# Loads on one ring, stores on another, and the variance moved ahead, in a wavelet pyramid on a group-normalised image

## The chip, the cores and the metric

The kernel runs on one core of a Trainium2 chip. The metric is device time in microseconds, lower is better: the median of three runs of the kernel before is 1376.59 us (1376.27 to 1378.16). The changed kernel is timed on the same chip beside it.

## The reference

The input `x` is float32 of shape 8 x 32 x 512 x 512. Each image is group-normalised with 16 groups, so that a group is two neighbouring channels: mean and variance over 2 x 512 x 512 elements, epsilon 1e-5. A three-level low-pass pyramid of the normalised image is added to `x`:

```python
def _wavelet_pyramid(x, levels=3):
    k1 = jnp.array([0.25, 0.5, 0.25])
    K = jnp.outer(k1, k1)[None, None]
    result = x
    for level in range(levels):
        sh, sw = (H // 2 ** level, W // 2 ** level)
        temp = result[:, :, :sh, :sw].reshape(B * C, 1, sh, sw)
        approx = conv(temp, K, stride 1, padding SAME)
        down = approx[:, :, ::2, ::2]
        result = result.at[:, :, :sh // 2, :sw // 2].set(down)
    return result

x = x + _wavelet_pyramid(_gn(x))
```

Each level smooths the top-left corner left by the level before with a 3 x 3 kernel, takes every second row and column, and writes that into the corner's own top-left quarter. Outside the 256 x 256 corner the output is therefore `x` plus its normalised self, a scaling by (1 + r) with a bias, where r is the reciprocal standard deviation; inside, `x` plus a level of the pyramid.

## The kernel before, in words

There are 128 groups of two channels (2.097 MB each). All of a group lies in one of eight slots of `xs` in SBUF: 128 partitions, each with eight rows of 512 elements (2 channels, 2 halves of the image called top and bottom, 2 rows per partition), ordered half first, then channel, then row. The groups run in laps of eight, one group a step. In step u an engine's program holds work of three groups: u itself, u - 1 (`LAG`) and u - 2 (`LAG_L3`). Each engine has its order written out by hand in its `step`, and semaphores tie the engines together.

SyncE (lines 131 to 159) carries all transfers on one ring, as DMAs of 1 MB, half a group each. At the start it issues the loads of all eight slots. Then for each group k: it waits until ScalarE has scaled the bottom half (`scaled`), stores it (L136), waits for the two VectorE additions (`l1_added`, `l2_added`), stores the top half (L139), and issues the two loads (L145) of the group six further on, once the slot's former group is stored.

VectorE, in its step: L309 forms 2 x even + odd columns of the new group into `h1` (semaphore `h1_part`); `rstd` (L273, L274) takes the reciprocal of the standard deviation of the group before and frees its variance bank; L315 adds the left neighbours into `h1` and accumulates the row sums (`h1_ready`); L321 adds row pairs into `a1`; `add_corner` (L296, twice) adds the pyramid's corner of group u - 2 out of PSUM; `add_level1` (L284 and L285) adds level 1 of group u - 1 at the right and below.

TensorE, in its step: `mean` (L346 to L348, which wait for `h1_ready`); `level3` of group u - 2 (L397 to L400); `level1` of group u, eight matmuls (L361 to L369); `variance` (L376), which needs ScalarE's sum of squares; `level2` of group u - 1 (L387 to L389). Matmuls are float32, and each of them shows as two records in the trace.

ScalarE, in its step: `moments` (L433 turns the mean in PSUM into the negative mean, L438 squares the whole group and accumulates), `evacuate1` (L449 and L450, level 1 from PSUM to `l1`), `root` (L458, standard deviation), `scale_beside` (L472) and `scale_bottom` (L477) of group u - 1, `evacuate2` (L465).

GpSimd refines r by one Newton step (`coefs`, L223 to L234), which gives the scaling's coefficients, and corrects the first column of `l1` after its evacuation (L256).

Of the kernel before, what the change touches and what calls it, by code (L numbers as in the profile page):

```python
# [16 lines left out]
SLOTS = 8  # L17
LAG = 1
LAG_L3 = 2
AHEAD = 6  # L20


def pyramid_kernel(nc: bass.Bass, x: bass.AP, out: bass.AP):
# [7 lines left out]


    def groups(a):
        return a.rearrange("b (g c) (f p s) w -> (b g) p c f (s w)", c=CG, f=HALVES, s=RPP)

    x_dram = groups(x).rearrange("(l k) p c f n -> l k f p c n", k=SLOTS)
    out_dram = groups(out).rearrange("(l k) p c f n -> l k f p c n", k=SLOTS)

    with ExitStack() as ctx:
        def sb(name, shape, dt=F32):  # L40
# [8 lines left out]

        xs = sb("xs", [P, SLOTS, ROWS * W])  # L50
        h1 = sb("h1", [P, 2, ROWS, W1])
        a1 = sb("a1", [P, 2, HALVES, CG, W1])
        l1 = sb("l1", [P, 2, CG, RPP, W1])
        l2 = sb("l2", [P, 2, CG, W2])
        squares = sb("squares", [P, ROWS * W], BF16)
# [69 lines left out]
        def rows(slot):  # L125
            return xs[:, slot, :].rearrange("p (r w) -> p r w", w=W)

        def half_of(slot, f):
            return xs[:, slot, :].rearrange("p (f c n) -> p f c n", c=CG, f=HALVES)[:, f]

        @block.sync
        def _(sp):
            def store(lap, k):
                n = lap * SLOTS + k
                sp.wait_ge(scaled, n + 1)
                sp.dma_start(out_dram[lap, k, 1], half_of(k, 1)).then_inc(x_stored[k], 16)  # L136
                sp.wait_ge(l1_added, n + 1)
                sp.wait_ge(l2_added, n + 1)
                sp.dma_start(out_dram[lap, k, 0], half_of(k, 0)).then_inc(x_stored[k], 16)  # L139

            def load(lap, slot):
                if later(lap, 0, 1):
                    sp.wait_ge(x_stored[slot], 16 * HALVES * lap)
                for f in range(HALVES):
                    sp.dma_start(half_of(slot, f), x_dram[lap, slot, f]).then_inc(x_loaded[slot], 16)  # L145

            def step(lap, k, last=False):
                store(lap, k)
                if later(lap * SLOTS, k, SLOTS - AHEAD) and not (last and k + AHEAD >= SLOTS):
                    load(lap + (k + AHEAD) // SLOTS, (k + AHEAD) % SLOTS)  # L150

            for k in range(SLOTS):
                load(0, k)
            for lap in range(LAPS):
                for k in range(SLOTS):
                    step(lap, k, last=lap == LAPS - 1)

            for slot in range(SLOTS):
                sp.wait_ge(x_stored[slot], 16 * HALVES * LAPS)

        @block.gpsimd
        def _(pool):
# [104 lines left out]
        def _(dve):  # L267
# [8 lines left out]
            def add_level1(base, k):  # L276
                b = k % 2
                d = slice(b, b + 1)
                top = rows(k % SLOTS)[:, 0:TOP]
                l1v = l1[:, b].rearrange("p c s w -> p (c s) w")  # L280
                dve.wait_ge(r_ready, base + k + 1)
                dve.wait_ge(l1_fixed, base + k + 1)
                right, below = top[:, :, W2:W1], top[HP:P, :, 0:W2]
                nc.vector.scalar_tensor_tensor(right, l1v[:, :, W2:W1], r[:, d], right, ALU.mult, ALU.add)  # L284
                nc.vector.scalar_tensor_tensor(below, l1v[HP:P, :, 0:W2], r[HP:P, d], below, ALU.mult,  # L285
                                               ALU.add).then_inc(l1_added, 1)

            def add_corner(base, k):
                b = k % 2
                d = slice(b, b + 1)  # L290
                img = rows(k % SLOTS)[:, 0:TOP].rearrange("p (c s) w -> p c s w", s=RPP)
                dve.wait_ge(l3_ps_ready, base + k + 1)
                for s in range(RPP):
                    level = l2_ps[b][HP * s:HP * (s + 1), 0:CG * W2].rearrange("p (c w) -> p c w", c=CG)
                    corner = img[0:HP, :, s, 0:W2]
                    last = nc.vector.scalar_tensor_tensor(corner, level, r[0:HP, d], corner, ALU.mult, ALU.add)  # L296
                last.then_inc(l2_added, 1)

            def step(lap, u):
                base = lap * SLOTS  # L300
                b = u % 2
                k = u - LAG
                make = exists(base, u)
                if make:
                    dve.wait_ge(x_loaded[u], 16 * HALVES * (lap + 1))
                    if later(base, u, 2):
                        dve.wait_ge(l1_ps_ready, base + u - 1)
                    v = rows(u)
                    nc.vector.scalar_tensor_tensor(h1[:, b], v[:, :, 0:W:2], 2.0, v[:, :, 1:W:2], ALU.mult,  # L309
                                                   ALU.add).then_inc(h1_part, 1)  # L310
                if exists(base, k):
                    rstd(base, k)
                if make:
                    dve.wait_ge(h1_part, base + u + 1)
                    nc.vector.scalar_tensor_tensor(h1[:, b, :, 1:W1], v[:, :, 1:W - 2:2], 1.0, h1[:, b, :, 1:W1],  # L315
                                                   ALU.mult, ALU.add,
                                                   accum_out=hsum[:, b:b + 1]).then_inc(h1_ready, 1)
                    dve.wait_ge(h1_ready, base + u + 1)
                    hp = h1[:, b].rearrange("p (i s) w -> p i s w", s=RPP)
                    av = a1[:, b].rearrange("p f c w -> p (f c) w")  # L320
                    nc.vector.scalar_tensor_tensor(av, hp[:, :, 0], 2.0, hp[:, :, 1], ALU.mult,  # L321
                                                   ALU.add).then_inc(a1_ready, 1)
                if exists(base, u - LAG_L3):
                    add_corner(base, u - LAG_L3)
                if exists(base, k):
                    add_level1(base, k)
# [10 lines left out]
        def _(pe):  # L337
            pe.wait_ge(consts_ready, 1)

            def mean(base, u):  # L340
                b = u % 2
                pe.wait_ge(h1_ready, base + u + 1)
                if later(base, u, 1):
                    pe.wait_ge(negm_ready, base + u)
                dst = mean_ps[:, 0:ROWS]
                nc.tensor.matmul(dst, mean_w[:], h1[:, b, :, 0], start=True, stop=False)  # L346
                nc.tensor.matmul(dst, mean_w[:], rows(u)[:, :, W - 1], start=False, stop=False)  # L347
                nc.tensor.matmul(mean_ps[:, 0:1], mean_w[:], hsum[:, b:b + 1], start=False,  # L348
                                 stop=True).then_inc(mean_ready, 1)

            def level1(base, u):
                b = u % 2
                hv = h1[:, b].rearrange("p (f c s) w -> p f c s w", f=HALVES, s=RPP)
                av = a1[:, b]
                even, odd = l1_ps[b][:, 0], l1_ps[b][:, 1]
                even_t, even_b, odd_t, odd_b = even[0:HP], even[HP:P], odd[0:HP], odd[HP:P]
                prev, mid, nxt = w1_prev[:, 0:HP], w1_even[:, 0:HP], w1_odd[:, 0:HP]
# [8 lines left out]
                nc.tensor.matmul(odd_b, mid, hv[:, 1, :, 1], start=True, stop=False)  # L366
                nc.tensor.matmul(odd_t, nxt, av[:, 0], start=False, stop=True)  # L367
                nc.tensor.matmul(even_b, mid, av[:, 1], start=False, stop=True)  # L368
                nc.tensor.matmul(odd_b, nxt, av[:, 1], start=False, stop=True).then_inc(l1_ps_ready, 1)  # L369

            def variance(base, u):
# [31 lines left out]
            def step(lap, u):  # L403
                base = lap * SLOTS
                if exists(base, u):
                    mean(base, u)
                if exists(base, u - LAG_L3):
                    level3(base, u - LAG_L3)
                if exists(base, u):
                    level1(base, u)  # L410
                    variance(base, u)
                if exists(base, u - LAG):
                    level2(base, u - LAG)

# [9 lines left out]
        def _(act):  # L424
# [43 lines left out]
            def scale_beside(base, k):  # L468
                c = slice(k % 2, k % 2 + 1)
                act.wait_ge(coef_ready, base + k + 1)  # L470
                beside = rows(k % SLOTS)[:, 0:TOP, W1:W]
                nc.scalar.activation(beside, beside, ACT.Identity, bias=negmr[:, c], scale=r_plus1[:, c])  # L472

            def scale_bottom(base, k):
                c = slice(k % 2, k % 2 + 1)
                bottom = xs[:, k % SLOTS, TOP * W:ROWS * W]
                nc.scalar.activation(bottom, bottom, ACT.Identity, bias=negmr[:, c],  # L477
                                     scale=r_plus1[:, c]).then_inc(scaled, 1)

            def step(lap, u):  # L480
                base = lap * SLOTS
                make, done = exists(base, u), exists(base, u - LAG)
                if make:
                    moments(base, u)
                    evacuate1(base, u)
                    root(base, u)
                if done:
                    scale_beside(base, u - LAG)
                    scale_bottom(base, u - LAG)
                    evacuate2(base, u - LAG)  # L490

            for lap, u in HEAD:
                step(lap, u)
# [19 lines left out]
```

## Time and profile before

| | |
|---|---|
| median of three runs | 1376.59 us |
| the profiled execution, its own time | 1377.61 us |
| its span (first to last instruction) | 1375.9 us |
| moved by DMA | 537.08 MB, 390 GB/s over the span |
| packets | 139280; 131072 of 4 KB carry the data |
| granted TensorE clock, mean | 0.996 |

The busy time of an engine as a share of the span says how full it is, not whether it is the limit. A wait names the engine that waited, the line it was about to run, and the instruction that ended the wait. The chain of waits is followed back from the last instruction, so an engine that shows on it in a stretch set the pace there. The windows give for a stretch each engine's busy time with its number of instructions, the granted clock, the mean busy share of the 16 DMA engines (it can be a little over 1, because packets of an engine overlap slightly) and the GB/s they moved.

### The profile page before, as it was taken

How to read it: one execution, taken by the hardware profiler on the slowest of the kernel's cores; microseconds unless marked ns; L12 is line 12 of the kernel's file. 1: busy time of each engine (PE TensorE's matmuls, PEld its weight loads, DVE VectorE, ACT ScalarE, POOL GpSimd, SP SyncE). 2: the span in 40 equal slices, each digit the busy share in tenths (PEclk: the TensorE clock that was granted, in tenths of full speed). 3: DMA queues.
4: the chain of work that ended last, by engine and by line, in shares of the span. 5: the costliest groups of instructions: out<-in, count | busy, mean ns of one | idle time of the engine just before them, and what ended most of it. 6: DMA issues, size and time to landing. Idle time of an engine off the chain costs nothing.

```text
span 1375.9 us, 18859 instructions
## 1 busy us (share of the span) xinstructions
PE 1229.0 (89%) x5632; PEld 692.5 (50%) x5632; DVE 1077.1 (78%) x1280; ACT 1138.6 (83%) x1282; POOL 598.7 (44%) x1316
## 2 busy tenths in 40 slices
PE   4989998998999899989989998999899899989997
PEld 1555455455545554554555455555545554555554
DVE  4787877878787878778787878787787878787874
ACT  3888888888888888888888888888888888888886
POOL 4444444444444444444444444444444444444442
PEclk9999999999999999999999999999999999999999
DMA  9799999999999999999999999999999999999976
GB/s 382 300 401 398 401 395 401 399 398 401 398 403 394 403 398 399 397 401 398 397 401 400 402 394 402 400 399 398 401 400 397 401 399 400 397 400 398 400 316 244
DMA packets 139280, 537.08 MB, mean 390 GB/s; under 512 B 8192, under 2 KB 8192, under 8 KB 139264
## 3 DMA queue, kind: packets, MB, share of 16 engines
q1 hardware_dynamic: 139264, 536.90, 99.6%
q8 instruction: 5, 0.08, 0.0%
q14 instruction: 11, 0.09, 0.0%
HBM read 268.44 MB, written 268.44 MB: 390 GB/s over the span
## 4 chain that ended last, share of the span: by engine, by line
PE 60%; DVE 23%; ACT 9%; issue 7%; DMA 1%; ACTq 0%; DVEq 0%; SPq 0%
DVE h L315 20%; PE l_ps L362 9%; PE l_ps L361 8%; PE l_ps L369 8%; PE l_ps L365 8%; PE l_ps L367 8%; ACT l L450 6%; PE l_ps L397 4%; PE mean_ps L346 4%; PE l_ps L398 2%; PE mean_ps L347 2%; PE l_ps L399 2%; PE l_ps L400 2%; PE mean_ps L348 2%; ACT std L458 2%
## 5 line engine op out<-in xcount | busy, mean ns | idle before, releaser
L438 ACT ACTIVATE squares<-xs,negm 128x4096 bf16<-128x4096 f32 x128 | 475.0, 3711 | 4.2
L256 POOL TENSOR_TENSOR l<-l,col_fix 128x4 f32<-128x4 f32 x128 | 28.3, 221 | 688.4 <-ACT l L450 688.4
L309 DVE SCALAR_TENSOR_TENSOR h<-xs 128x2048 f32<-128x2048 f32 x128 | 293.7, 2295 | 12.2 <-DMA xs<-x_dram 8.3
L315 DVE SCALAR_TENSOR_TENSOR h<-xs,h 128x2040 f32<-128x2040 f32 x128 | 291.0, 2274 | 0.0
L223 POOL TENSOR_TENSOR newt<-r 128x1 f32<-128x1 f32 x128 | 270.5, 2113 | 37.1 <-DVE ve L274 37.1
L477 ACT ACTIVATE xs<-xs,negmr,r_plus 128x2048 f32<-128x2048 f32 x128 | 268.0, 2094 | 0.0
L449 ACT ACTIVATE l<-l_ps,negm_e 128x512 f32<-128x512 f32 x128 | 87.9, 687 | 190.3 <-PE l_ps L369 190.3
L296 DVE SCALAR_TENSOR_TENSOR xs<-l_ps,r,xs 64x256 f32<-64x256 f32 x256 | 123.0, 480 | 109.6 <-PE l_ps L400 107.8
L346 PE MATMUL mean_ps<-h,mean_w 128*128 128x8 f32 x256 | 50.1, 268 | 138.1 <-DVE h L315 138.1
L321 DVE SCALAR_TENSOR_TENSOR a<-h 128x1024 f32<-128x1024 f32 x128 | 157.0, 1227 | 4.4
L472 ACT ACTIVATE xs<-xs,negmr,r_plus 128x1024 f32<-128x1024 f32 x128 | 159.7, 1247 | 0.0
L273 DVE RECIPROCAL r<-std 128x1 f32<-128x1 f32 x128 | 21.0, 164 | 162.8 <-ACT std L458 162.8
L226 POOL TENSOR_TENSOR newt<-newt,ve 128x1 f32<-128x1 f32 x128 | 147.8, 1154 | 0.0
L362 PE MATMUL l_ps<-h,w_even 128*64 128x512 f32 x256 | 139.0, 625 | 0.0
L363 PE MATMUL l_ps<-h,w_prev 128*64 128x512 f32 x256 | 139.0, 625 | 0.0
L346 PEld LDWEIGHTS mean_ps<-h,mean_w 128*128 128x128 f32 x256 | 38.5, 189 | 191.1 <-DVE h L315 178.1
L361 PE MATMUL l_ps<-h,w_prev 128*128 128x512 f32 x256 | 133.1, 602 | 0.0
L365 PE MATMUL l_ps<-a,w_even 128*64 128x512 f32 x256 | 131.9, 597 | 0.0
L366 PE MATMUL l_ps<-h,w_even 128*64 128x512 f32 x256 | 131.8, 597 | 0.0
L367 PE MATMUL l_ps<-a,w_odd 128*64 128x512 f32 x256 | 130.7, 592 | 0.0
L368 PE MATMUL l_ps<-a,w_even 128*64 128x512 f32 x256 | 130.7, 592 | 0.0
L369 PE MATMUL l_ps<-a,w_odd 128*64 128x512 f32 x256 | 130.7, 592 | 0.0
(83 smaller groups left out, 2300.6 us busy)
## 6 DMA issues: line engine op xcount, KB each, us to landing
xs<-x_dram SPq DMA_DIRECT2D x256, 1024.0 KB, 10.4
y_dram<-xs SPq DMA_DIRECT2D x256, 1024.0 KB, 7.3
```

Of the source, the lines that this page charges most:

```text
L223: nc.gpsimd.tensor_tensor(newt[:, b, 0:1], r0[:, c], r0[:, c], ALU.mult).then_inc(newt_step, 1)
L309: nc.vector.scalar_tensor_tensor(h1[:, b], v[:, :, 0:W:2], 2.0, v[:, :, 1:W:2], ALU.mult, ALU.add).then_inc(h1_part, 1)
L315: nc.vector.scalar_tensor_tensor(h1[:, b, :, 1:W1], v[:, :, 1:W - 2:2], 1.0, h1[:, b, :, 1:W1], ALU.mult, ALU.add, accum_out=hsum[:, b:b + ...
L321: nc.vector.scalar_tensor_tensor(av, hp[:, :, 0], 2.0, hp[:, :, 1], ALU.mult, ALU.add).then_inc(a1_ready, 1)
L361: nc.tensor.matmul(even, w1_prev[:], hv[:, 0, :, 1], start=True, stop=False)
L362: nc.tensor.matmul(odd_t, mid, hv[:, 0, :, 1], start=True, stop=False)
L365: nc.tensor.matmul(even_t, mid, av[:, 0], start=False, stop=True)
L367: nc.tensor.matmul(odd_t, nxt, av[:, 0], start=False, stop=True)
L369: nc.tensor.matmul(odd_b, nxt, av[:, 1], start=False, stop=True).then_inc(l1_ps_ready, 1)
L438: nc.scalar.activation(squares[:], xs[:, u % SLOTS, :], ACT.Square, bias=negm[:, b:b + 1], accum_out=sumsq[:, b:b + 1]).then_inc(sumsq_rea ...
L472: nc.scalar.activation(beside, beside, ACT.Identity, bias=negmr[:, c], scale=r_plus1[:, c])
L477: nc.scalar.activation(bottom, bottom, ACT.Identity, bias=negmr[:, c], scale=r_plus1[:, c]).then_inc(scaled, 1)
```

## The change

All loads stay on SyncE's ring, and a group is loaded by one DMA of 2 MB; SyncE does nothing else. A group is stored by one DMA of 2 MB, which ScalarE issues on its own ring at the end of its step, two steps after the group's load was used; it waits for the scaling and both VectorE additions. The rows in a slot are ordered channel first, then half, then row, as in DRAM, so views of a half are now strided and `add_level1` needs two instructions where it had one. On TensorE the variance matmul goes ahead of the last level 1 matmul, and two of the three mean lines wait for `h1_part` in place of `h1_ready`. On ScalarE the scaling beside and the root go ahead of `evacuate1`.

```diff
-        return a.rearrange("b (g c) (f p s) w -> (b g) p c f (s w)", c=CG, f=HALVES, s=RPP)
+        return a.rearrange("b (g c) (f p s) w -> (b g) p (c f) (s w)", c=CG, f=HALVES, s=RPP)
...
-        a1 = sb("a1", [P, 2, HALVES, CG, W1])
+        a1 = sb("a1", [P, 2, CG, HALVES, W1])
...
+        def top_of(slot):
+            return xs[:, slot, :].rearrange("p (c f s w) -> p f c s w", c=CG, f=HALVES, s=RPP)[:, 0]
+        def whole(slot):
+            return xs[:, slot, :].rearrange("p (h n) -> p h n", n=RPP * W)
...
         def _(sp):
...
             def load(lap, slot):
                 if later(lap, 0, 1):
-                    sp.wait_ge(x_stored[slot], 16 * HALVES * lap)
-                for f in range(HALVES):
-                    sp.dma_start(half_of(slot, f), x_dram[lap, slot, f]).then_inc(x_loaded[slot], 16)
+                    sp.wait_ge(x_stored[slot], 16 * lap)
+                sp.dma_start(whole(slot), x_dram[lap, slot]).then_inc(x_loaded[slot], 16)
             for lap in range(LAPS):
-                for k in range(SLOTS):
-                    step(lap, k, last=lap == LAPS - 1)
+                for slot in range(SLOTS):
+                    load(lap, slot)
...
             def add_level1(base, k):
...
-                nc.vector.scalar_tensor_tensor(right, l1v[:, :, W2:W1], r[:, d], right, ALU.mult, ALU.add)
-                nc.vector.scalar_tensor_tensor(below, l1v[HP:P, :, 0:W2], r[HP:P, d], below, ALU.mult,
-                                               ALU.add).then_inc(l1_added, 1)
+                for s in range(RPP):
+                    right = top[:, :, s, W2:W1]
+                    nc.vector.scalar_tensor_tensor(right, l1v[:, :, s, W2:W1], r[:, d], right, ALU.mult, ALU.add)
+                for s in range(RPP):
+                    below = top[HP:P, :, s, 0:W2]
+                    last = nc.vector.scalar_tensor_tensor(below, l1v[HP:P, :, s, 0:W2], r[HP:P, d], below, ALU.mult,
+                                                          ALU.add)
+                last.then_inc(l1_added, 1)
...
             def mean(base, u):
                 b = u % 2
-                pe.wait_ge(h1_ready, base + u + 1)
+                pe.wait_ge(h1_part, base + u + 1)
...
                 nc.tensor.matmul(dst, mean_w[:], rows(u)[:, :, W - 1], start=False, stop=False)
+                pe.wait_ge(h1_ready, base + u + 1)
                 nc.tensor.matmul(mean_ps[:, 0:1], mean_w[:], hsum[:, b:b + 1], start=False,
...
                 nc.tensor.matmul(even_b, mid, av[:, 1], start=False, stop=True)
+                variance(base, u)
                 nc.tensor.matmul(odd_b, nxt, av[:, 1], start=False, stop=True).then_inc(l1_ps_ready, 1)
...
                     level1(base, u)
-                    variance(base, u)
...
+            def store(lap, k):
+                n = lap * SLOTS + k
+                slot, back = k % SLOTS, k // SLOTS
+                act.wait_ge(scaled, n + 1)
+                act.wait_ge(l1_added, n + 1)
+                act.wait_ge(l2_added, n + 1)
+                nc.scalar.dma_start(out_dram[lap + back, slot], whole(slot)).then_inc(x_stored[slot], 16)
...
                 if make:
                     moments(base, u)
-                    evacuate1(base, u)
-                    root(base, u)
                 if done:
                     scale_beside(base, u - LAG)
+                if make:
+                    root(base, u)
+                    evacuate1(base, u)
+                if done:
                     scale_bottom(base, u - LAG)
                     evacuate2(base, u - LAG)
+                if exists(base, u - LAG_L3):
+                    store(lap, u - LAG_L3)
```

## Rows read from the trace of the kernel before

**Rows 1.** The page: busy time of the engines, and the DMA queue.
```profile
PE 1229.0 (89%) x5632; PEld 692.5 (50%) x5632; DVE 1077.1 (78%) x1280; ACT 1138.6 (83%) x1282; POOL 598.7 (44%) x1316
...
q1 hardware_dynamic: 139264, 536.90, 99.6%
```

**Rows 2.** The waits: who waited for whom, us in total, times, longest.
```profile
ACT l L449 <- PE l_ps L369: 190.3, 128, 2.8
DVE r L273 <- ACT std L458: 162.8, 128, 8.0
PE mean_ps L346 <- DVE h L315: 138.1, 128, 13.1
DVE h L309 <- DMA xs<-x_dram: 8.3, 1, 8.3
```

**Rows 3.** The chain of waits over one period: start us, us, what.
```profile
698.97 2.21 DVE h L315 x2
...
701.22 0.39 PE mean_ps L346 x2
701.61 0.22 PE mean_ps L347 x2
701.83 0.22 PE mean_ps L348 x2
702.05 0.48 PE l_ps L397 x2
...
706.79 0.87 PE l_ps L369 x2
...
708.27 0.68 ACT l L450
708.96 0.16 ACT std L458
...
709.48 2.21 DVE h L315 x2
```

**Rows 4.** The timeline of the same period: start us, us, engine, line.
```profile
702.39 3.71 ACT L438 ACTIVATE squares<-xs,negm 128x4096 bf16<-128x4096 f32 x1
...
708.84 0.26 ACT L458 ACTIVATE std<-var_ps,eps_t 128x1 f32<-128x1 f32 x1
708.99 1.25 ACT L472 ACTIVATE xs<-xs,negmr,r_plus 128x1024 f32<-128x1024 f32 x1
...
710.18 0.61 PE L389 MATMUL l_ps<-l,w_second 128*128 128x254 f32 x2
```

**Rows 5.** Groups of instructions: two VectorE additions, busy us and mean ns.
```profile
L296 DVE SCALAR_TENSOR_TENSOR xs<-l_ps,r,xs 64x256 f32<-64x256 f32 x256 | 123.0, 480 | 109.6 <-PE l_ps L400 107.8
...
L284 DVE SCALAR_TENSOR_TENSOR xs<-l,r,xs 128x512 f32<-128x512 f32 x128 | 94.4, 737 | 0.6 <-POOL r L231 0.6
```

**Rows 6.** Windows; the last three numbers are PEclk, DMA share and GB/s.
```profile
0.00:5.00 5.00, 0.00 (x0) 0.00 (x0) 0.00 (x0) 0.00 (x0) 3.44 (x25) 1.00 0.62 209
...
20.00:25.00 5.00, 1.77 (x8) 0.57 (x4) 0.61 (x3) 2.81 (x4) 0.42 (x2) 1.00 1.03 410
...
55.00:60.00 5.00, 4.40 (x18) 2.54 (x15) 3.82 (x4) 3.70 (x5) 2.04 (x2) 1.00 0.29 112
...
100.00:400.00 300.00, 272.32 (x1259) 154.08 (x1259) 240.65 (x288) 254.15 (x286) 133.95 (x289) 1.00 1.02 399
...
600.00:602.00 2.00, 2.00 (x12) 0.56 (x6) 1.97 (x2) 1.13 (x2) 0.00 (x0) 1.00 1.03 422
602.00:604.00 2.00, 2.00 (x10) 1.29 (x9) 0.92 (x1) 1.37 (x4) 0.00 (x0) 1.00 1.00 344
...
1365.00:1370.00 5.00, 3.97 (x21) 2.98 (x20) 2.88 (x6) 2.37 (x3) 0.00 (x0) 1.00 1.02 403
```

**Rows 7.** Instructions by line: duration ns min/median/max, first and last start.
```profile
L315 DVE SCALAR_TENSOR_TENSOR h<-xs,h x128: 2272/2273/2283, 10.6 to 1350.3; 128x2040 f32<-128x2040 f32 x128
...
L136 SPq DMA_DIRECT2D y_dram<-xs x128: 372/383/388, 39.8 to 1367.0; - x128
...
L145 SPq DMA_DIRECT2D xs<-x_dram x256: 435/932/5488, 0.8 to 1314.6; - x128
```

More of the change, by code:

```diff
@@ L19 @@
 LAG_L3 = 2
-AHEAD = 6
 def pyramid_kernel(nc: bass.Bass, x: bass.AP, out: bass.AP):
@@ L33, in groups @@
     def groups(a):
-        return a.rearrange("b (g c) (f p s) w -> (b g) p c f (s w)", c=CG, f=HALVES, s=RPP)
-    x_dram = groups(x).rearrange("(l k) p c f n -> l k f p c n", k=SLOTS)
-    out_dram = groups(out).rearrange("(l k) p c f n -> l k f p c n", k=SLOTS)
+        return a.rearrange("b (g c) (f p s) w -> (b g) p (c f) (s w)", c=CG, f=HALVES, s=RPP)
+    x_dram = groups(x).rearrange("(l k) p h n -> l k p h n", k=SLOTS)
+    out_dram = groups(out).rearrange("(l k) p h n -> l k p h n", k=SLOTS)
     with ExitStack() as ctx:
@@ L128, in half_of @@
         def half_of(slot, f):
-            return xs[:, slot, :].rearrange("p (f c n) -> p f c n", c=CG, f=HALVES)[:, f]
+            return xs[:, slot, :].rearrange("p (c f n) -> p f c n", c=CG, f=HALVES)[:, f]
+        def top_of(slot):
+            return xs[:, slot, :].rearrange("p (c f s w) -> p f c s w", c=CG, f=HALVES, s=RPP)[:, 0]
+        def whole(slot):
+            return xs[:, slot, :].rearrange("p (h n) -> p h n", n=RPP * W)
         @block.sync
         def _(sp):
[L133 to L139, printed above, removed]
             def load(lap, slot):
                 if later(lap, 0, 1):
-                    sp.wait_ge(x_stored[slot], 16 * HALVES * lap)
-                for f in range(HALVES):
-                    sp.dma_start(half_of(slot, f), x_dram[lap, slot, f]).then_inc(x_loaded[slot], 16)
[L147 to L150, printed above, removed]
-            for k in range(SLOTS):
-                load(0, k)
+                    sp.wait_ge(x_stored[slot], 16 * lap)
+                sp.dma_start(whole(slot), x_dram[lap, slot]).then_inc(x_loaded[slot], 16)
             for lap in range(LAPS):
-                for k in range(SLOTS):
-                    step(lap, k, last=lap == LAPS - 1)
+                for slot in range(SLOTS):
+                    load(lap, slot)
             for slot in range(SLOTS):
-                sp.wait_ge(x_stored[slot], 16 * HALVES * LAPS)
+                sp.wait_ge(x_stored[slot], 16 * LAPS)
         @block.gpsimd
@@ L278, in add_level1 @@
                 d = slice(b, b + 1)
-                top = rows(k % SLOTS)[:, 0:TOP]
-                l1v = l1[:, b].rearrange("p c s w -> p (c s) w")
+                top, l1v = top_of(k % SLOTS), l1[:, b]
                 dve.wait_ge(r_ready, base + k + 1)
                 dve.wait_ge(l1_fixed, base + k + 1)
-                right, below = top[:, :, W2:W1], top[HP:P, :, 0:W2]
-                nc.vector.scalar_tensor_tensor(right, l1v[:, :, W2:W1], r[:, d], right, ALU.mult, ALU.add)
-                nc.vector.scalar_tensor_tensor(below, l1v[HP:P, :, 0:W2], r[HP:P, d], below, ALU.mult,
-                                               ALU.add).then_inc(l1_added, 1)
+                for s in range(RPP):
[6 more added lines that the diff above has]
+                last.then_inc(l1_added, 1)
             def add_corner(base, k):
@@ L290, in add_corner @@
                 d = slice(b, b + 1)
-                img = rows(k % SLOTS)[:, 0:TOP].rearrange("p (c s) w -> p c s w", s=RPP)
+                img = top_of(k % SLOTS)
                 dve.wait_ge(l3_ps_ready, base + k + 1)
@@ L304, in step @@
                 if make:
-                    dve.wait_ge(x_loaded[u], 16 * HALVES * (lap + 1))
+                    dve.wait_ge(x_loaded[u], 16 * (lap + 1))
                     if later(base, u, 2):
@@ L319, in step @@
                     hp = h1[:, b].rearrange("p (i s) w -> p i s w", s=RPP)
-                    av = a1[:, b].rearrange("p f c w -> p (f c) w")
+                    av = a1[:, b].rearrange("p c f w -> p (c f) w")
                     nc.vector.scalar_tensor_tensor(av, hp[:, :, 0], 2.0, hp[:, :, 1], ALU.mult,
@@ L352, in level1 @@
                 b = u % 2
-                hv = h1[:, b].rearrange("p (f c s) w -> p f c s w", f=HALVES, s=RPP)
-                av = a1[:, b]
+                hv = h1[:, b].rearrange("p (c f s) w -> p f c s w", f=HALVES, s=RPP)
+                av = a1[:, b].rearrange("p c f w -> p f c w")
                 even, odd = l1_ps[b][:, 0], l1_ps[b][:, 1]
@@ L470, in scale_beside @@
                 act.wait_ge(coef_ready, base + k + 1)
-                beside = rows(k % SLOTS)[:, 0:TOP, W1:W]
+                beside = top_of(k % SLOTS)[:, :, :, W1:W]
                 nc.scalar.activation(beside, beside, ACT.Identity, bias=negmr[:, c], scale=r_plus1[:, c])
@@ L475, in scale_bottom @@
                 c = slice(k % 2, k % 2 + 1)
-                bottom = xs[:, k % SLOTS, TOP * W:ROWS * W]
+                bottom = half_of(k % SLOTS, 1)
                 nc.scalar.activation(bottom, bottom, ACT.Identity, bias=negmr[:, c],
                                      scale=r_plus1[:, c]).then_inc(scaled, 1)
+            def store(lap, k):
[5 more added lines that the diff above has]
+                nc.scalar.dma_start(out_dram[lap + back, slot], whole(slot)).then_inc(x_stored[slot], 16)
             def step(lap, u):
```

## The prediction

> **What bounds the kernel now.** I read the page first: TensorE is busy 89% of the span, ScalarE 83%, VectorE 78%, and the one DMA queue 99.6% [rows 1]. Two suspects, then: a chain of compute, and the DMA engines. The waits come next, because a bound by loads would show there. VectorE waited for a load once, 8.3 us at the start, and never again; what it, TensorE and ScalarE wait for in every one of the 128 groups is each other [rows 2]. The chain of waits says how: from one L315 to the next it runs through mean, level 3, level 1 on TensorE, then both evacuations (the last is L450) and the root on ScalarE, the reciprocal on VectorE, and back to L315. The two L315 rows stand 10.51 us apart, and no DMA is in between [rows 3]. First and last L315 start at 10.6 and 1350.3 us [rows 7]; 127 periods of 10.51 are 1334.8, so the ramp costs 4.9 more, and 25.6 us follow the last start to the span's 1375.9.
>
> So compute sets the pace. The windows show how little the DMA engines have in reserve, which is the heart of this prediction. A group moves 2.097 MB in and as much out, 4.194 MB. In the steady stretch they move 399 GB/s, that is 10.51 us a group: exactly compute's period. Loads alone ran at 410, stores alone (the end of the run) at 403, the best 2 us windows between at 422, and once a period there is a dip to 344 [rows 6]. Whether 399 is what compute asks for or nearly all that mixed traffic can get, the trace of before cannot tell.
>
> **The change on the compute side.** Two of the three mean matmul lines wait only for L309's half: after L315 there is one line (0.39) where there were 0.39 + 0.22 + 0.22 before level 3 [rows 3], so 0.44 us leaves the chain. The variance matmul goes ahead of L369 and the root ahead of the evacuations. In the times of [rows 3, 4]: squares end at 702.39 + 3.71, plus 0.1 for the accumulator read, 706.2; less 0.44 that is 705.8. TensorE reaches L369's place at 706.79 - 0.44 = 706.35, so the variance waits for nothing and ends near 706.75. ScalarE meanwhile does the scaling beside (1.25 us, to 707.0), then the root (0.26), and the reciprocal pair (0.35) frees L315 at 707.65 in place of 709.48. The chain is 1.83 us shorter: 8.7 us. The scaling needs GpSimd's coefficients of the group before; GpSimd works 598.7/128 = 4.7 us a group [rows 1], and counted from a root one period back it is done some 3 us before ScalarE asks. Its own wait for the evacuation comes behind that and costs nobody.
>
> What is late next is each engine's own work. TensorE: from L346 at 701.22 to the end of L389 at 710.79 without a pause, **9.57 us**; the moved matmuls stay in that sum. ScalarE: a period of 10.51 less its wait of 190.3/128 = 1.49 [rows 2] is 9.02, and now it issues the stores. One issue of 1 MB on SyncE took 0.37 to 0.39 us; the loads' issues 0.44 at least, 0.93 in the median and 5.49 at most, where the ring was full [rows 7]. For a store of 2 MB I take 0.4 to 0.9, by the store rows and the median, as one 2 MB store a period should find room: 9.4 to 9.95. The store's three waits are for work of the step before and of VectorE, finished early; behind it in ScalarE's order stand the next moments, which need a mean that comes no sooner. VectorE: 1077.1/128 = 8.41 us [rows 1], plus the split additions. A 512-element addition takes 737 ns, one of 256 takes 480 [rows 5], so two pairs for two singles cost 2 x (960 - 737) = 0.45: 8.86, covered by TensorE's 9.57. SyncE loses all waits but that for a free slot, and nothing is queued behind its loads. The new slot order leaves every matmul and scaling its element count and only changes strides; I cost it at nothing. Should strides cost, what hides it is the room between compute's period and DMA's, below, some 0.5 us a group. Taken together compute's period is 9.6 to 9.95, I say **9.8**. Were it alone, the span would be 10.6 + 4.9 + 127 x 9.8 + 30.6 = 1291, where 30.6 is the tail of 25.6 plus 5: the last two stores go out whole behind ScalarE's last step, 2 MB more than now wait at that point.
>
> **The change on the DMA side.** The bytes stay. At 9.8 us a group the engines would have to move 428 GB/s, above every row. So DMA becomes the bound, and compute has slack it can't use. The price of a group is not shown for two rings that mix loads with stores packet by packet; it is bounded by the rows: 4.194 MB at 422 is 9.94 us, at 399 it is 10.51, and a loss by mixing could exceed that. Half the bytes are loads (410), half stores (403): 10.23 and 10.41, mean **10.32 us**, which I take because each of the two is held over a whole stretch with the queue full, while 422 is a peak of 2 us and 399 may be no more than what compute asks for; the ends stay for the range.
>
> To 128 x 10.32 = 1321 comes the time in which the engines have nothing to do. Start: 5 us at 209 in place of 410 [rows 6], 2.4. Ramp: eight loads of 5.1 end at 43.4; the first store now goes at the end of the third step, about 39.8 [rows 7] + 9.8 + 0.4 = 50, since it is sent whole after the corner; 6.6 empty. Then the ninth load waits for that store to land, some 2 us empty, shrinking each period by the 0.5 that DMA is slower than compute: 6 in all. (Before has its own hole here, 112 GB/s at 55 to 60.) Tail: from the last load's landing L309's 2.3 and then the 30.6 plus a wait, 34, in which three stores fill 15: 19 empty. Sum 34, span 1321 + 34 = **1355**. The profiled execution was 1377.6, 1.7 above its span, and the median of the runs is 1376.6, 1.0 below that: 1355 + 1.7 - 1.0 = about **1355 us**, 1.5% below before.
>
> **Weighed against a rule.** The steady row has 399 GB/s with one ring [rows 6]. The Trainium skill (DMA: Bandwidth & Descriptors, Rules for kernel authors) says that spreading DMAs over several issuing engines doesn't help bandwidth, as all run on the same 16 DMA engines and interleave. By it the sum is the first rival's; the trace bears it out in so far as the queue's busy share is already 99.6% [rows 1], and contradicts nothing, since no row has two rings.
>
> **Rivals.**
> *The mixed rate stays where it is.* If 399 is the ceiling of mixed traffic, a group costs 10.51 whatever compute does: 128 x 10.51 + 34 = 1379, about no change, the compute gain swallowed whole. For it: busy share 99.6%, the dip in every period. Against it: between dips windows reach 422, and compute alone explains 10.51. The Trainium skill's rule above speaks for it.
>
> *The rings mix badly (slower).* Each DMA engine now alternates between reading and writing HBM; before it did 1 MB of one, then 1 MB of the other. The break-even is a group of (1376 - 34)/128 = 10.48 us, 400 GB/s. If the whole of a period ran like the mean of the dip window and the steady rate, (344 + 399)/2 = 372, a group would take 11.27: 1477; with a quarter of that loss, 392, it is 10.70: 1403. For it: 400 is hardly above today's rate. Against: loads following stores show no loss but that dip.
>
> *The two rings overlap better.* If mixed traffic runs at the 422 of the best windows, DMA needs 128 x 9.94 + 34 = 1306 and compute's 1291 lies just under it: 1291 to 1320. For it: those windows are themselves mixed or change over between kinds. Against: no stretch longer than a few us holds it.
>
> *ScalarE's issue blocks.* Stores on ScalarE's queue hold its activations while the ring is full. It decides from 10.51 - 9.02 = 1.5 us per issue; at 2 us it is 11.02 a group, 10.6 + 4.9 + 127 x 11.02 + 30.6 = 1446, and at 5.49 in every group 14.5, 1888. Against: a ring took several 1 MB loads at once, and here one store is in flight.
>
> **How the numbers follow.** Forecast, DMA-bound at 401 to 412 GB/s, 1338 to 1372: 0.45. Better overlap, below 1338: 0.22. Rate unchanged, 1372 to 1384: 0.15. Bad mixing: 0.14. Blocked issue: 0.04. A measurement here can tell about 0.2%, 2.8 us, from no change. Faster by more than that takes the first two and a fifth of the third, 0.70; within it 0.10; slower gets the rest, 0.20. The range from 1308 to 1390 leaves out a twentieth below and some 0.12 above.
>
> **What would show it.** Right: L273's wait for the root and L346's for L315 shrink to near nothing; loads by 2 MB; the steady windows at 403 to 410 GB/s; in the later part of the run VectorE's L309 waiting for loads in place of compute's old chain, some tenths of a us a group. Compute-bound near 9.8: no such waits, windows at 420 or over. Wrong: steady windows at or under 399 with many L309 waits (rings), or gaps on ScalarE at the store's issue (blocked), or TensorE still waiting for L315 with 10.5 us between (the chain was not cut).

## The result, and the profile after

The changed kernel takes 1305.39 us in the median (1304.38 to 1306.31), before 1377.38 in the same session: a ratio of 0.9477, 95% interval 0.9461 to 0.9493. That is faster, as forecast, but by 5.2% where 1.5% was predicted, and 2.6 us under the lower end of the range. The prediction is wrong.

The page of the changed kernel, busy time and the two DMA rings, against [rows 1]:

```profile
PE 1227.1 (94%) x5632; PEld 700.1 (54%) x5632; DVE 1100.6 (84%) x1536; ACT 1139.1 (87%) x1282; POOL 599.7 (46%) x1316
...
q1 hardware_dynamic: 67584, 268.44, 50.9%
q10 hardware_dynamic: 67584, 268.44, 50.2%
...
xs<-x_dram SPq DMA_DIRECT2D x128, 2048.0 KB, 16.4
y_dram<-xs ACTq DMA_DIRECT2D x128, 2048.0 KB, 29.7
```

TensorE does the same work in 72 us less. The last two lines give the median time from issue to landing: a store now needs 29.7 us, three periods, so that some three stores are on their way at a time.

The waits of the changed kernel, against [rows 2]:

```profile
DVE h L303 <- DMA xs<-x_dram: 101.5, 79, 8.7
...
ACT l L445 <- PE l_ps L366: 69.0, 127, 0.7
...
PE mean_ps L344 <- DVE h L309: 45.5, 79, 2.1
...
DVE r L264 <- ACT std L454: 6.3, 3, 4.3
```

The old chain is gone: VectorE's wait for the root fell from 162.8 us to 6.3 and comes three times. In its place it waits for loads (L303 is the former L309), in 79 of 128 groups. Which 79, the starts of L303 show; two stretches of its row, first and last start in each, and under the second the wait that stands beside it (us, times):

```profile
L303 DVE SCALAR_TENSOR_TENSOR h<-xs x5: 2292/2293/2293, 299.6 to 338.3; 128x2048 f32<-128x2048 f32 x5
...
L303 DVE SCALAR_TENSOR_TENSOR h<-xs x5: 2293/2293/2299, 999.2 to 1039.6; 128x2048 f32<-128x2048 f32 x5
...
  DMA xs<-x_dram: 6.0, 5
```

Five starts are four periods: 38.7 / 4 = 9.68 us early on, 40.4 / 4 = 10.10 later. In the first stretch no wait for a load stands beside the row, in the second there are five. But for the very first group, whose load has to come in, the waits begin with the 51st. So the kernel is bound by compute for its first 50 groups, while the loads' lead over compute is used up, and by DMA from then on. The windows, against [rows 6]:

```profile
0.00:5.00 5.00, 0.00 (x0) 0.00 (x0) 0.00 (x0) 0.00 (x0) 3.45 (x25) 1.00 0.53 184
...
40.00:60.00 20.00, 19.73 (x91) 11.22 (x91) 17.84 (x27) 18.08 (x21) 7.22 (x20) 1.00 0.86 313
60.00:100.00 40.00, 39.45 (x183) 22.91 (x182) 35.68 (x50) 36.87 (x43) 14.53 (x41) 1.00 1.02 398
...
400.00:700.00 300.00, 288.02 (x1331) 165.17 (x1329) 258.34 (x361) 267.85 (x301) 143.31 (x302) 1.00 1.02 421
700.00:1000.00 300.00, 283.23 (x1306) 161.06 (x1305) 254.75 (x358) 263.15 (x298) 158.41 (x299) 1.00 1.02 417
...
1270.00:1280.00 10.00, 9.46 (x46) 5.46 (x44) 8.51 (x13) 8.78 (x11) 5.38 (x10) 1.00 0.65 265
1280.00:1290.00 10.00, 9.30 (x42) 5.88 (x38) 3.29 (x9) 8.81 (x10) 1.40 (x8) 1.00 0.55 220
1290.00:1304.00 14.00, 1.21 (x9) 0.98 (x8) 1.00 (x3) 0.38 (x1) 0.00 (x0) 0.67 0.89 354
```

The engines move 421, later 417 GB/s, not the 406 of the forecast (4.194 MB in 10.32 us). The 421 lasts until some 700 us, longer than the lead of the loads; why it is 417 after that was not tried. The busy share beside it is 1.02, the very number that stood beside 399 in [rows 6].

Theories after the result: **A**, one ring that changes between loads and stores cannot carry more than about 399, and the two rings brought the rate; **B** (later called C), 399 was only what compute asked for, and one ring would have followed a faster compute as well.

### The profile page after: what moved, and what is told of

It is laid out like the page before. It is cut to its first block, busy times and chain, and to the rows that moved or that the text cites. A ratio compares the mean times of both kernels' runs of the same rounds, so it can differ in the third digit from the quotient of the medians.

```text
span 1304.0 us, 19101 instructions
## 1 busy us (share of the span) xinstructions
PE 1227.1 (94%) x5632; PEld 700.1 (54%) x5632; DVE 1100.6 (84%) x1536; ACT 1139.1 (87%) x1282; POOL 599.7 (46%) x1316
## 4 chain that ended last, share of the span: by engine, by line
DMA 47%; PE 30%; ACT 13%; issue 5%; DVE 3%; ACTq 1%; DVEq 0%
DMA y_dram<-xs 30%; DMA xs<-x_dram 17%; ACT xs L473 8%; PE l_ps L366 5%; PE l_ps L358 5%; PE l_ps L357 4%; PE l_ps L361 4%; PE l_ps L363 4%; ACT l L446 3%; DVE h L309 3%; PE l_ps L394 2%; PE var_ps L373 1%; ACTq L482 1%; PE l_ps L395 1%; PE l_ps L396 1%
## 5 line engine op out<-in xcount | busy, mean ns | idle before, releaser
L247 POOL TENSOR_TENSOR l<-l,col_fix 128x4 f32<-128x4 f32 x128 | 183.3, 1432 | 642.5 <-ACT l L446 642.5
L303 DVE SCALAR_TENSOR_TENSOR h<-xs 128x2048 f32<-128x2048 f32 x128 | 293.6, 2294 | 103.1 <-DMA xs<-x_dram 101.5
L309 DVE SCALAR_TENSOR_TENSOR h<-xs,h 128x2040 f32<-128x2040 f32 x128 | 291.5, 2277 | 0.0
L315 DVE SCALAR_TENSOR_TENSOR a<-h 128x1024 f32<-128x1024 f32 x128 | 157.4, 1229 | 4.4
L468 ACT ACTIVATE xs<-xs,negmr,r_plus 128x1024 f32<-128x1024 f32 x128 | 157.0, 1227 | 0.2 <-issue 0.2
L366 PE MATMUL l_ps<-a,w_odd 128*64 128x512 f32 x256 | 137.2, 618 | 0.0
L361 PE MATMUL l_ps<-a,w_even 128*64 128x512 f32 x256 | 131.8, 597 | 0.0
L363 PE MATMUL l_ps<-a,w_odd 128*64 128x512 f32 x256 | 130.7, 592 | 0.0
L215 POOL TENSOR_TENSOR newt<-r,half_t 128x1 f32<-128x1 f32 x128 | 122.1, 954 | 0.0
L278 DVE SCALAR_TENSOR_TENSOR xs<-l,r,xs 64x256 f32<-64x256 f32 x256 | 113.5, 485 | 1.9
L275 DVE SCALAR_TENSOR_TENSOR xs<-l,r,xs 128x256 f32<-128x256 f32 x256 | 111.3, 473 | 0.8 <-POOL r L222 0.8
L373 PEld LDWEIGHTS var_ps<-sumsq,var_w 128*128 128x128 f32 x256 | 38.1, 188 | 103.9 <-ACT squares L434 103.0
L384 PEld LDWEIGHTS l_ps<-l,w_first 128*128 128x128 f32 x256 | 38.1, 188 | 103.1 <-issue 103.1
## 6 DMA issues: line engine op xcount, KB each, us to landing
y_dram<-xs ACTq DMA_DIRECT2D x128, 2048.0 KB, 29.7
```

The costliest lines, as they stand in the source:

```text
L247: nc.gpsimd.tensor_tensor(col, col, col_fix[:, b], ALU.add).then_inc(l1_fixed, 1)
L361: nc.tensor.matmul(even_t, mid, av[:, 0], start=False, stop=True)
```

## The experiments

### Each half of the change alone

The compute order put into the kernel before, nothing else:

```diff
-                pe.wait_ge(h1_ready, base + u + 1)
+                pe.wait_ge(h1_part, base + u + 1)
...
+                pe.wait_ge(h1_ready, base + u + 1)
                 nc.tensor.matmul(mean_ps[:, 0:1], mean_w[:], hsum[:, b:b + 1], start=False,
...
+                variance(base, u)
                 nc.tensor.matmul(odd_b, nxt, av[:, 1], start=False, stop=True).then_inc(l1_ps_ready, 1)
...
                     moments(base, u)
-                    evacuate1(base, u)
-                    root(base, u)
                 if done:
                     scale_beside(base, u - LAG)
+                if make:
+                    root(base, u)
+                    evacuate1(base, u)
```

> The kernel before with the compute part of the change alone: variance ahead of the last level 1 matmul, root and scaling beside ahead of the evacuations, two mean lines waiting for the half; one ring, 1 MB DMAs, slot order and additions as before. Theory A (one ring that changes between loads and stores can carry no more than about 399 GB/s): the compute chain is cut, but the period stays at 10.4 to 10.5 us, 1360 to 1380 us, and VectorE begins to wait for loads. Theory B (399 was only what compute asked for, and the ring is not what matters): 415 GB/s or more, a period of 9.7 to 10.1, 1280 to 1320 us, as the full change.

Measured: 1309.04 us, ratio 0.951 (0.9496 to 0.9523). Its windows, on one ring of 1 MB DMAs:

```profile
200.00:300.00 100.00, 98.65 (x455) 55.47 (x453) 86.43 (x105) 92.24 (x103) 33.59 (x102) 1.00 1.02 421
...
900.00:1000.00 100.00, 93.64 (x436) 53.66 (x434) 81.88 (x100) 87.36 (x99) 60.32 (x100) 1.00 1.02 411
```

Theory B. The same ring that carried 399 carries 421 once compute asks for a group every 9.68 us, and nearly the whole gain is there without a second ring. TensorE is busy for 98.65 of these 100 us, so its own work has taken the place of the old chain.

The other half, the changed kernel with the old compute order on TensorE and ScalarE (the lines above the other way round):

> The changed kernel with the compute order of before (variance after level 1, evacuations ahead of the root and the scaling beside, mean waiting for the whole of h1): two rings, 2 MB DMAs, the new slot order and the split additions remain. Theory A and B agree: the old chain sets a period of 10.5, 1375 to 1385 us, with no wait for loads and 399 GB/s. A third theory (the stores' issue or the new slot order itself changes compute's period): clearly off that, over 1390 or under 1365.

Measured: 1382.52 us, ratio 1.0042 (1.0027 to 1.0056). As both theories had it; rings, 2 MB DMAs, slot order and split additions cost 0.4% where compute does not profit. Its steady windows read 398 to 402 GB/s with a busy share of 1.01 to 1.02, on two rings. Now the same number has come from one ring and from two at the same pace of compute.

### The transfers alone

All arithmetic is left out and a store waits for its load only. First with the kernel before's ring:

```diff
-                sp.wait_ge(scaled, n + 1)
+                sp.wait_ge(x_loaded[k], 16 * HALVES * (lap + 1))
                 sp.dma_start(out_dram[lap, k, 1], half_of(k, 1)).then_inc(x_stored[k], 16)
-                sp.wait_ge(l1_added, n + 1)
-                sp.wait_ge(l2_added, n + 1)
```

> The transfers of the kernel before alone: SyncE's one ring, 1 MB DMAs in the same order and slots, a store waiting only for its load; all arithmetic is left out and the input is copied. Theory C (the engines carry about 421 GB/s on one ring whenever enough is queued, and 399 was compute's demand): 415 to 422 GB/s, 1280 to 1300 us. Theory A (one ring that changes between loads and stores has its ceiling near 399): 1345 to 1365 us.

then with the changed kernel's two, ScalarE's whole program being

```python
for n in range(G):
    k = n % SLOTS
    act.wait_ge(x_loaded[k], 16 * (n // SLOTS + 1))
    act.dma_start(out_dram[n // SLOTS, k], whole(k)).then_inc(x_stored[k], 16)
```

> The transfers of the changed kernel alone: loads on SyncE's ring, stores on ScalarE's, 2 MB each, a store waiting only for its load; all arithmetic is left out and the input is copied. Theory C: 418 to 422 GB/s as on one ring, 1280 to 1295 us. If mixing on two rings has a price or a gain of its own, it stands here as the difference to the copy on one ring, over 5 us.

Measured: 1284.59 us on one ring, 1280.83 on two, one execution each. Two windows of the copy on one ring:

```profile
5.00:30.00 25.00, 0.00 (x0) 1.00 1.03 411
...
400.00:1200.00 800.00, 0.00 (x0) 1.00 1.03 421
```

and one of the copy on two:

```profile
400.00:1200.00 800.00, 0.00 (x0) 1.00 1.02 422
```

(no engine has work in them, so few columns are left: busy POOL, PEclk, DMA share, GB/s). This is the ceiling, 421 to 422 GB/s, with loads and stores mixed, on either. Mixing has no price that shows: the copy on one ring runs at 411 from 5 to 30 us, with hardly anything but loads, the mix after it at 421. Two rings gain 3.8 us, 0.3%, in one execution each.

### Size and number of rings in the changed kernel

```diff
-                sp.dma_start(whole(slot), x_dram[lap, slot]).then_inc(x_loaded[slot], 16)
+                for c in range(CG):
+                    h = slice(HALVES * c, HALVES * (c + 1))
+                    sp.dma_start(whole(slot)[:, h], x_dram[lap, slot, :, h]).then_inc(x_loaded[slot], 16)
...
```

(the store likewise, the waits doubled)

> The changed kernel with each 2 MB DMA cut into two of 1 MB (one per channel), still on two rings. If the two rings brought the rate: 1300 to 1310 us, 416 to 421 GB/s, no change to the changed kernel. If the size of the DMA brought it: back towards 399 to 410 GB/s, 1325 to 1380.

Measured: 1308.57 us, ratio 0.9503 (0.949 to 0.9517), 420 GB/s and later 412 to 417. The size of the DMA brought nothing that shows.

The stores back on SyncE's ring, but 2 MB each:

```diff
+            for n in range(G):
+                store(n // SLOTS, n % SLOTS)
+                m = n + AHEAD
+                if SLOTS <= m < G:
+                    load(m // SLOTS, m % SLOTS)
```

> The changed kernel with the stores moved back to SyncE's ring, 2 MB each, in the order of before (store of a group, then the load six groups ahead); compute order, slot order and additions as changed. Theory A (one ring is the limit): 399 to 405 GB/s and 1345 to 1380 us, with VectorE waiting for loads. Theory B (ring count does not matter): 1300 to 1315.

Measured: 1343.71 to 1371.53 us in four runs, median 1360.11; the ratio, 0.9797 (0.976 to 0.9833), counts the two shortest, 1343.71 and 1353.59. Between the theories, and inconclusive. Two windows of the run of 1366.64 us, the only one with a trace:

```profile
300.00:400.00 100.00, 98.62 (x453) 56.64 (x453) 89.15 (x124) 91.51 (x105) 36.63 (x101) 1.00 1.02 421
...
1000.00:1100.00 100.00, 89.62 (x387) 48.54 (x385) 75.15 (x106) 79.25 (x88) 51.10 (x88) 0.95 0.97 369
```

For the first half it runs at 421 like the others, so the ring itself carries it. Loads come late from the 49th group on, and the rate still holds 421 to some 700 us; then it falls, to some 370 in the end. The granted clock falls too, to 0.95 on average, but after the rate, which read 409 and 403 GB/s between 740 and 760 us at a clock of 1.00. In this order a load stands behind a store that SyncE may issue only when compute is done, and compute then waits for that load; I think the ring runs low there, but that was not tried. Why nearly the same order in 1 MB pieces keeps 411 stays open. One difference is that there the bottom half of a group leaves as soon as it is scaled (L136), ahead of the two additions for which the whole store waits here.

### Which move shortened the period

Variance, root and scaling beside moved, the mean left as before (the first experiment's diff without its first two parts):

> The kernel before with only the variance, the root and the scaling beside moved ahead; the three mean lines still wait for the whole of h1. The chain loses 1.83 - 0.44 = 1.4 us, to 9.1, under TensorE's own 9.57. Theory C: compute's period 9.6 to 9.9, then DMA's 10.1, 1305 to 1315 us, all of the gain. If the mean's move is needed too (TensorE waits for h1 with nothing before it to do): 10.0 to 10.2, 1320 to 1345.

Measured: 1309.22 us, ratio 0.951 (0.9485 to 0.9536): the whole gain. The mean's two lines alone (those two parts only):

> The kernel before with only the two mean lines moved ahead to wait for the half. The old chain loses 0.44 us: a period of 10.07, about DMA's own. Theory C: 46 + 127 x 10.07 = 1325 us, between 1318 and 1332, and 412 to 418 GB/s on the one ring. If DMA were the bound of before: no change, 1370 to 1378.

Measured: 1376.27 us, ratio 0.9991 (0.9982 to 1.0001): nothing, where 1325 was expected. The chain of waits of this kernel, one period, tells why:

```profile
689.94 0.39 ACT l L466
690.33 0.04 issue
690.37 0.49 PE l_ps L398 x2
...
691.54 0.86 PE l_ps L362 x2
...
695.12 0.87 PE l_ps L370 x2
...
696.61 0.68 ACT l L451
697.28 0.15 ACT std L459
697.44 1.13 ACT xs L473
698.56 0.62 ACT xs L478
...
700.44 0.39 ACT l L466
```

It is another loop than that of [rows 3]: level 1 on TensorE, the evacuations, then the root and both scalings on ScalarE, its second evacuation (L466 here, L465 before), and level 3, which needs it, back to level 1 (this kernel's line numbers are one higher than before's from L348 on). 700.44 - 689.94 = 10.50 us, with no mean and no L315 in it. Two loops of almost one length, then. Each was cut by itself. The scaling beside alone (it leaves only the second loop):

```diff
                     moments(base, u)
+                if done:
+                    scale_beside(base, u - LAG)
+                if make:
                     evacuate1(base, u)
                     root(base, u)
                 if done:
-                    scale_beside(base, u - LAG)
```

> The kernel before with only the scaling beside moved ahead of the evacuations; variance, root and mean as before. Theory of two loops of equal length (loop 1: level 1 matmuls, evacuations, root, reciprocal, L315, mean, level 3; loop 2: level 1 matmuls, evacuations, scalings, the second evacuation L465, level 3): this shortens only loop 2, loop 1 keeps 10.5 us, 1370 to 1380 us. Theory of one loop through the scalings: 9.7 to 10.1, 1305 to 1325.

Measured: 1360.4 us, ratio 0.9871 (0.9856 to 0.9886), a little better than "no change". Its chain is the first loop again:

```profile
691.20 2.21 DVE h L315 x2
...
694.28 0.34 PE l_ps L397 x2
...
701.56 2.21 DVE h L315 x2
```

10.36 us, and the 0.15 that it lost stands in one row: L397 takes 0.34 on the chain where it took 0.48 in [rows 3]. Those 0.14 us had been the second loop's: level 3 waited for L465 there. The timeline of the kernel before has it:

```profile
701.60 0.38 ACT L465 ACTIVATE l<-l_ps 128x256 f32<-128x256 f32 x1
...
701.66 0.30 PEld L348 LDWEIGHTS mean_ps<-hsum,mean_w 128*128 128x128 f32 x2
...
702.03 0.30 PEld L397 LDWEIGHTS l_ps<-l,w_even 128*128 128x128 f32 x2
```

L465 ends at 701.98, and the weights of L397 are loaded from 702.03, 0.37 us behind those of L348; here it is 0.23 us. Alone the first loop is 10.36 long, the second 10.50.

Variance and root moved ahead, the scaling beside left behind the evacuations (it cuts only the first loop):

```diff
                     moments(base, u)
-                    evacuate1(base, u)
                     root(base, u)
+                    evacuate1(base, u)
```

> The kernel before with only the variance and the root moved ahead; the scaling beside stays behind the evacuations, mean as before. Theory of two loops: loop 1 is cut to 9.1, but loop 2 loses only the root's 0.15 on ScalarE and gains the variance's 0.25 on TensorE ahead of L369: 10.4 to 10.65 us a group, 1365 to 1395 us. Theory of loop 1 alone, as the prediction had it: 9.7 to 10.1, 1305 to 1325.

Measured: 1477.92 us, ratio 1.0726 (1.0709 to 1.0742): a loss of 7%, where 10.4 to 10.65 us a group had been expected. Two of its windows:

```profile
100.00:400.00 300.00, 265.87 (x1171) 149.18 (x1171) 220.71 (x264) 236.46 (x268) 87.70 (x270) 0.95 0.98 371
...
694.00:695.00 1.00, 1.00 (x4) 0.36 (x2) 0.71 (x2) 1.00 (x1) 0.00 (x0) 0.50 1.02 422
```

and rows of its chain of waits over two neighbouring groups (the level 1 matmul L361 in each, and what lies between two evacuations L450):

```profile
694.23 1.71 PE l_ps L361 x2
...
701.12 0.69 ACT l L450
...
706.40 0.86 PE l_ps L361 x2
...
709.99 0.31 PE var_ps L377 x2
710.30 1.02 PE l_ps L370 x2
...
711.93 0.68 ACT l L450
```

Two things add up. Where the clock is full, from one L450 to the next it is 711.93 - 701.12 = 10.81 us: the second loop's 10.50 less the root's 0.15, plus 0.31 for the variance and the 0.15 by which L370 (L369 before) has grown, 1.02 for 0.87. So the loop through L465 holds with the clock left out, and the expectation had priced the variance too low. The rest is the clock: it averages 0.95, and where it falls TensorE runs at the lower of its two levels, 1.2 in place of 2.4 GHz, so that the same L361 takes 1.71 us in one group and 0.86 in the next. TensorE is on the loop, so the slow matmuls lengthen it further, to 12.0 us in some groups. What set the clock off was not tried: TensorE stood still for L465 ahead of level 3, 161.6 us in all or 1.26 a group, about as long in the group in which the clock then fell as in the next, in which it did not; its wait for L315 in the kernel before is 138.1 [rows 2], and there the clock stayed at 0.996.

### A version that beats both, and the changed kernel again

The empty time of the ramp and the late loads both suggest sending stores sooner: the two VectorE additions a store waits for are long done at the end of ScalarE's step.

```diff
                 if make:
                     moments(base, u)
+                if exists(base, u - LAG_L3):
+                    store(lap, u - LAG_L3)
...
                     evacuate2(base, u - LAG)
-                if exists(base, u - LAG_L3):
-                    store(lap, u - LAG_L3)
```

> The changed kernel with ScalarE's store issued right after the moments, ahead of the scaling beside, in place of the end of the step; the two additions it waits for are done by then. Every store goes out some 5 us earlier: up to 4 us less of empty DMA engines in the ramp, and more slack before loads are late. 1299 to 1304 us. If the wait for VectorE holds ScalarE there: over 1306.

> The changed kernel once more, on the chip of this call, to compare with the earlier store: 1303 to 1307 us, VectorE's waits for loads from about the 49th group on.

Measured: 1297.6 us, ratio 0.9422 (0.9409 to 0.9434), against 1306.59 and 0.9482 (0.9469 to 0.9495) for the changed kernel on the same chip: 9 us better, twice what was expected. Its windows:

```profile
40.00:60.00 20.00, 19.72 (x93) 11.44 (x92) 17.84 (x25) 18.45 (x23) 7.18 (x20) 1.00 1.02 411
...
400.00:700.00 300.00, 295.69 (x1365) 169.13 (x1364) 266.53 (x373) 275.80 (x311) 111.34 (x311) 1.00 1.02 421
700.00:1000.00 300.00, 286.90 (x1302) 163.12 (x1302) 254.34 (x357) 261.74 (x296) 124.59 (x300) 0.98 1.02 421
```

The hole of the ramp is closed (411 for 313 GB/s: 5 us), and the stretch from 700 to 1000 us keeps 421 where the changed kernel had 417. It has a price, which its waits show:

```profile
ACT xs L468 <- issue: 44.7, 36, 2.5
```

In 36 groups ScalarE stands before the scaling beside, 44.7 us in all, while its sequencer issues the store, which takes 4.36 us at most where the changed kernel's took 0.45. That is the prediction's rival of the blocked issue, here in the fastest kernel. Above the copy's 1281 us only 17 are left.

## Why the prediction was wrong, point by point

**What bounds before.** It was right that compute set the pace and no load did: cutting compute alone gives 0.951. But the prediction followed only the loop that the chain of waits drew. A second, through L465 and level 3, was as long (10.50 against 10.36 by itself); it touched the first at L397, 0.14 us, and showed in the waits hardly at all. The move priced at 0.44 us (mean) is worth nothing by itself, and the 1.83 us would not have come from variance and root without the scaling beside. The sum came out because the change cuts both.

**Compute's period.** 9.8 forecast, 9.68 measured. Split additions: 2 x 473 + 2 x 485 ns for 737 + 752 make 0.43, forecast 0.45. ScalarE's store issue: 0.38 to 0.45 us, at the lower end of the 0.4 to 0.9 forecast and never blocked, though some three stores were on their way and not the one that the rival assumed; in this kernel that rival fell.

**The rate: the step that failed.** "Half the bytes are loads (410), half stores (403): 10.23 and 10.41, mean 10.32 us." Measured, the transfers alone run at 421 to 422, 9.96 us. The step that failed is to take the rate of the mix for the mean of its parts. The 410 came from the first 40 us, with loads alone, and the copy has 411 there too; the 403 came from a tail in which each store ran alone; the mix runs above both. The 422 put down as "a peak of 2 us" was the ceiling. That is most of the miss: with 421 for the first half and 417 after it, less some 21 us of emptiness, a group took (1304 - 21) / 128 = 10.02, and 128 x (10.32 - 10.02) = 38 us.

**The empty time.** 34 us forecast. From the windows, against 421: start 2.8, 40 to 100 us 7.3, the end from 1270 us 10.7, together 21. The first store went out at 43.4 us where the forecast had 50, and at the end the stores still queued fill some of what was booked as empty (10.7 us against 19): 13 us, the rest of the miss of 51.

**The rivals.** The number of "the two rings overlap better", 1306, is the one that came true, for a reason that isn't its own: one ring does the same. "The mixed rate stays" and "the rings mix badly" fell with the copies. The rule quoted from the Trainium skill (DMA: Bandwidth & Descriptors, Rules for kernel authors), that spreading DMAs over issuing engines does not help bandwidth, holds here: 421 on one ring, 422 on two, and the changed kernel's 0.9477 against 0.951 for one ring, intervals that only just part. What was wrong was the rival hung on it, that the rate of before was therefore a ceiling. The busy share of 99.6% that spoke for it says little: the share is 1.02 at 399 and at 421 alike.

**The range.** It missed by 2.6 us of 1305. The rival of the better overlap had the right rate and the sum of 1306, but the range began at 1308, above that sum, and its chance was set at 0.22: the right case was on the page and got too little room.

## What to carry to other kernels

Before you call a rate the ceiling of the DMA engines, ask what pace the consumer sets: a period that compute explains to 0.1 us, as here, speaks for demand, and a copy without the compute can tell. When the chain of waits shows a loop, look for loops of nearly its length through the same instructions (here it showed as 0.14 us at a single matmul), and cut all of them in one change; half of a cut can be worth nothing or less. A store moved from the end of the step to where its waits are over gained 9 us here, although its issue then held ScalarE in some groups, so both have to be weighed.

## What the runs showed of the hardware that was not expected

The busy share of the DMA engines was no gauge here of what they could still carry. It is 1.02 at 399 GB/s [rows 6], 1.02 at 421 in the changed kernel, and 0.98 at 371 with variance and root alone. What they can carry showed only where more was asked for, in the copies and behind a faster compute. And a reordering that moved TensorE's wait to another place changed its clock: with variance and root alone ahead the granted clock fell from 0.996 to 0.95 on average, some level 1 matmuls took twice their time, and the run lost 7%, part of it by the clock.
